# The last of four batches ranked by comparing all pairs, and new orders on all engines

## What is computed

```python
x = L0_attn_x
x = x + _L0_attn_ref(_layernorm(x), Wq, bq, Wk, bk, Wv, bv, Wo, bo, gamma, beta)
x = x + _L0_ffn_ref(_layernorm(x), w_router, w_block)
# _L0_attn_ref(x): q = elu(x@Wq+bq)+1; k = elu(x@Wk+bk)+1, each head of k divided by its norm;
#   per head (q k^T) v; y = x + attn@Wo + bo; layernorm(y)*gamma + beta
# _L0_ffn_ref(x), per batch of 1024 tokens:
scores = einsum('bld,d->bl', x, w_router)
_, top_idx = top_k(scores, 768)                 # ties: the earlier token wins
out = x.at[b, top_idx].set(gelu(x[b, top_idx] @ w_block))
```

## Time and profile before

| | us |
|---|---|
| median of 3 runs (lowest, highest) | 93.24 (93.05, 93.5) |
| the profiled execution | 93.43 |
| its span, first to last instruction | 91.7 |
| outside the span | 1.73 |
| busy: PE, DVE, ACT, POOL | 78.3, 77.8, 63.6, 65.6 |
| mean granted clock of PE | 0.884 |

### The profile page before, as it was taken

One profiled execution on the slowest core, in us unless ns is written; L12 is line 12 of the kernel. 1 busy time (PEld: TensorE's weight loads), 2 busy tenths in 40 slices (PEclk: granted clock), 3 DMA queues, 4 the chain that ended last, 5 costly groups with the idle time before them and its releaser, 6 DMA issues.

```text
span 91.7 us, 2510 instructions
## 1 busy us (share of the span) xinstructions
PE 78.3 (85%) x846; PEld 65.8 (72%) x846; DVE 77.8 (85%) x281; ACT 63.6 (69%) x187; POOL 65.6 (72%) x133
## 2 busy tenths in 40 slices
PE   4997995999999999999999999999995479985400
PEld 1356674669969979979999899989883368773300
DVE  4376999696598999999997999778879999999970
ACT  5004689999999949834998496696689997970000
POOL 5678769579799998888598888768589998600000
PEclk9999999999999999999999999999998555555555
DMA  1968979500059999993000000000000000006395
GB/s 33 283 157 298 336 275 422 223 4 7 4 63 138 139 130 131 142 145 40 0 0 7 0 0 0 0 0 11 0 0 11 0 0 0 7 0 229 123 374 199
DMA packets 8643, 9.02 MB, mean 98 GB/s; under 512 B 819, under 2 KB 6326, under 8 KB 8630
## 3 DMA queue, kind: packets, MB, share of 16 engines
q0 software_dynamic: 4160, 2.10, 21.2%
q1 hardware_dynamic: 3888, 6.49, 20.2%
q10 hardware_dynamic: 582, 0.26, 1.0%
HBM read 4.66 MB, written 2.10 MB: 74 GB/s over the span
## 4 chain that ended last, share of the span: by engine, by line
PE 48%; POOL 18%; DVE 10%; ACT 8%; DMA 6%; issue 3%; ACTq 2%; DVEq 1%
POOL x_sb L455 8%; PE bank L1251 7%; PE bank L1294 6%; PE bank L1257 6%; PE bank L1267 6%; PE bank L1295 6%; DMA off_bo<-in_L_attn_bo_dram 6%; PE bank L1317 5%; ACT norm_sb L645 5%; DVE x_sb L968 4%; POOL r L436 3%; PE bank L1219 3%; PE bank L1306 3%; POOL r L421 2%; PE bank L1335 1%
## 5 line engine op out<-in xcount | busy, mean ns | idle before, releaser
L645 ACT ACTIVATE norm_sb<-xb_sb,shift,gain 128x128 f32<-128x128 f32 x32 | 12.9, 494 | 0.5 <-POOL shift L445 0.5
L1294 PE MATMUL bank<-M_sb,qT 128*128 128x128 f32 x64 | 12.5, 277 | 0.0
L1295 PE MATMUL bank<-back,hT 128*128 128x128 f32 x64 | 12.4, 275 | 0.0
L1335 PE MATMUL bank<-ones,reach 128*16 128x1 bf16 x256 | 10.2, 164 | 1.0 <-DVE reach L922 1.0
L637 ACT ACTIVATE x_sb<-bank,r 128x128 f32<-128x128 f32 x32 | 9.7, 375 | 1.7 <-DVE s_col L897 1.6
L1344 PE MATMUL bank<-rise,rise_by 33*128 33x16 bf16 x96 | 7.0, 175 | 4.1 <-DVE rise L934 3.8
L455 POOL TENSOR_TENSOR x_sb<-x_sb,xb_sb 128x512 f32<-128x512 f32 x8 | 10.0, 1266 | 0.0
L1294 PEld LDWEIGHTS bank<-M_sb,qT 128*128 128x128 f32 x64 | 9.7, 192 | 0.2 <-ACT M_sb L606 0.2
L1317 PE MATMUL bank<-wz_c,hT 128*128 128x129 f32 x64 | 9.7, 285 | 0.0
L1295 PEld LDWEIGHTS bank<-back,hT 128*128 128x128 f32 x64 | 9.7, 192 | 0.0
L1335 PEld LDWEIGHTS bank<-ones,reach 128*16 128x16 bf16 x256 | 7.7, 88 | 2.4 <-DVE reach L922 1.3
(11 more groups left out here) (150 smaller groups left out, 216.0 us busy)
## 6 DMA issues: line engine op xcount, KB each, us to landing
xb_sb<-in_L_attn_x_dram SPq DMA_DIRECT2D x4, 512.0 KB, 7.7
xb_sb<-beta_sb POOLq DMA_DIRECT2D x4, 512.0 KB, 9.5
x_sb<-in_L_attn_x_dram SPq DMA_DIRECT2D x7, 256.0 KB, 5.9
out_dram<-x_sb SPq DMA_DIRECT2D x7, 256.0 KB, 2.4
x_sb<-in_L_attn_x_dram SPq DMA_DIRECT2D x2, 128.0 KB, 2.7
out_dram<-x_sb ACTq DMA_DIRECT2D x1, 128.0 KB, 2.5
out_dram<-x_sb SPq DMA_DIRECT2D x1, 128.0 KB, 2.5
w_sb<-in_L_attn_Wq_dram ACTq DMA_DIRECT2D x1, 64.0 KB, 2.6
```

Source lines behind the costliest of these rows:

```text
L645: last = nc.scalar.activation(norm_sb[:, t], xb_sb[:, t], ACT.Identity, bias=shift3[:, t:t + 1], scale=gain3[:, t:t + 1])
L1294: nc.tensor.matmul(o, qT[:, u, t * P:(t + 1) * P], M_sb[:, b], start=True, stop=False)
L1295: last = nc.tensor.matmul(o, hT[:, u, t * P:(t + 1) * P], back[:], start=False, stop=True)
L1335: last = nc.tensor.matmul(counts_of(s, i)[:, b - b0:b - b0 + 1], reach[:, T * b + t, :], ones16[:, 0:1], start=(t == 0), stop=(t == T - 1))
```

## The change

The diff has 1,310 lines, most of them the four rewritten lists and the banks. Its core:

```diff
-    NORM1 = "DDDDAAAA"
-    Y_STATS = "DDDAAAAA"
-    KEYS_BY = "PPPPDDPP"
+    NORM1 = "DDDDDDAA"
+    Y_STATS = "AAAAAAAA"
+    KEYS_BY = "PDPDPDPD"
...
-    RANK_SETS = ((0,), (1,), (2,), (3,))
-    ROOT_GROUPS = ((1,), (2,), (3,), (4, 5), (6, 7))
-    BUSY = 14
+    SUM_GROUPS = ((0, 1), (2, 3), (4, 5), (6,), (7,))
+    RANK_SETS = ((0,), (1,), (2,))
+    ROOT_GROUPS = ((1,), (2, 3), (4, 5), (6, 7))
+    BUSY = 11
+    def tokens(ap, b):
+        return ap[b].rearrange("(t p) d -> p t d", p=P) if b == LAST else ap[b].rearrange("(p t) d -> p t d", t=T)
+    x_v, out_v = [tokens(x, b) for b in range(B)], [tokens(out, b) for b in range(B)]
...
-            sp.dma_start(wz_sb[:, P:P + 1], w_router.unsqueeze(1)).then_inc(wz_in, 16)
             for b in range(B):
                 sp.dma_start(xb_sb[:, T * b:T * b + T, :], x_v[b]).then_inc(xb_in[b], 16)
+                if b == 0:
+                    sp.wait_ge(bo_room, 1)
+                    sp.dma_start(off_bo[:, D - 1:D], bo.unsqueeze(1)).then_inc(bo_in, 16)
+            sp.dma_start(wz_sb[:, P:P + 1], w_router.unsqueeze(1)).then_inc(wz_in, 16)
...
+            def rank_counts():
+                nc.gpsimd.memset(rise[:], 0.0)
+                nc.gpsimd.iota(lanes_i[:], pattern=[[0, B], [1, LANES]], base=0, channel_multiplier=0)
...
...
-            act.wait_ge(bo_room, 1)
-            act.dma_start(off_bo[:, D - 1:D], bo.unsqueeze(1)).then_inc(bo_in, 16)
+            def copy_s_row(h):
+                act.wait_ge(s_full, h + 1)
+                nc.scalar.copy(s_row[:, HW * h:HW * h + HW], bank_of(("s", h))).then_inc(s_row_done, 1)
+            def copy_sums(h):
+                act.wait_ge(sums_full, h + 1)
+                nc.scalar.copy(part_sums[:, HW * h:HW * h + HW], bank_of(("sums", h))).then_inc(sums_done, 1)
...
+            def compare(J, part):
+                c0, c1 = (P * (J + 1), HW) if part == 0 else (max(P * (J + 1), HW), T * P)
+                dve.wait_ge(s_row_done, part + 1)
+                nc.vector.tensor_scalar(beats[:, J, c0:c1], s_row[:, c0:c1], s_col[:, T * LAST + J:T * LAST + J + 1], None,
+                                        ALU.is_le).then_inc(beats_done, 1)
+            def compare_own(h):
+                for I in range(TH * h, TH * h + TH):
+                    last = nc.vector.scalar_tensor_tensor(out=beats[:, I, I * P:(I + 1) * P], in0=s_row[:, I * P:(I + 1) * P],
+                                                          scalar=s_col[:, T * LAST + I:T * LAST + I + 1], in1=later16[:],
+                                                          op0=ALU.is_le, op1=ALU.mult)
...
+            def score_rows(h):
+                pe.wait_ge(s_col_done, 4 * LAST + 2 * h + 2)
...
+                for t in range(TH):
+                    n = T * LAST + TH * h + t
+                    last = nc.tensor.transpose(o[:, t * P:(t + 1) * P], s_col[:, n:n + 1].to_broadcast([P, P]), ident[:])
+            def row_sums(h):
+                pe.wait_ge(beats_done, 10 if h else 7)
+                pe.wait_ge(own_done, 2)
+                for n in range(TH):
+                    J = TH * h + n
+                    for I in range(J, T):
+                        last = nc.tensor.matmul(o[:, n * P:(n + 1) * P], beats[:, J, I * P:(I + 1) * P], ident16[:],
+                                                start=(I == J), stop=(I == T - 1))
+                last.then_inc(sums_full, 1)
+            def place_columns(h):
...
+                pe.wait_ge(beats_done, 10 if h else 3)
+                pe.wait_ge(own_done, h + 1)
...
+                for n in range(TH):
+                    for J in range(a + n + 1):
+                        nc.tensor.matmul(o[:, n:n + 1], beats[:, J, (a + n) * P:(a + n + 1) * P], ones16[:, 0:1],
+                                         start=False, stop=False)
+            def place_rows(h):
+                pe.wait_ge(sums_done, h + 1)
...
+                    last = nc.tensor.matmul(o[:, n:n + 1], part_sums[:, i * P:(i + 1) * P], minus16[:], start=False,
+                                            stop=(n == TH - 1))
```

More of the change, by code:

```diff
@@ L462, in add_x1 @@
                                         ALU.add).then_inc(added, 1)
+            head_masks()
             first_masks()
-            back_masks()
             first_roots(0)
@@ L1055, in _ @@
-            y_gamma(5)
-            x1_stats(3)
-            score_cols(1, 0)
-            mask_vk(3)
-            residual(4)
-            score_cols(1, 1)
-            split_keys(0)
-            x1_stats(4)
+            score_cols(1, 0)
+            x1_stats(3)
+            mask_vk(3)
+            score_cols(1, 1)
+            residual(4)
+            split_keys(0)
+            reach_lanes(0, 0)
+            x1_stats(4)
+            y_gamma(5)
             score_cols(2, 0)
-            reach_lanes(0, 0)
+            rise_lanes(0, 0)
@@ new lines, in _ @@
+            residual(7)
+            rise_lanes(2, 0)
+            rise_lanes(0, 2)
+            reach_lanes(1, 2)
+            reach_lanes(2, 1)
+            reach_lanes(0, 3)
+            rise_lanes(1, 2)
+            score_cols(6, 0)
+            score_cols(6, 1)
+            rise_lanes(2, 1)
+            rise_lanes(0, 3)
+            reach_lanes(1, 3)
+            reach_lanes(2, 2)
+            reach_lanes(0, 4)
+            rise_lanes(1, 3)
+            rise_lanes(2, 2)
+            rise_lanes(0, 4)
@@ L1103, in _ @@
+            reach_lanes(1, 4)
+            reach_lanes(2, 3)
+            reach_lanes(0, 5)
+            rise_lanes(1, 4)
+            rise_lanes(2, 3)
+            x1_stats(7)
+            reach_lanes(2, 4)
+            reach_lanes(1, 5)
+            rise_lanes(0, 5)
+            compare_own(0)
+            low_keys(0)
+            rise_lanes(2, 4)
+            rise_lanes(1, 5)
+            reach_lanes(0, 6)
+            compare(0, 0)
             score_cols(7, 0)
-            reach_lanes(1, 3)
@@ L1135, in _ @@
+            compare(1, 1)
+            compare(2, 1)
+            low_keys(2)
+            reach_lanes(1, 7)
             rise_lanes(0, 7)
-            rise_lanes(2, 5)
-            reach_lanes(1, 7)
-            rise_lanes(3, 3)
+            reach_lanes(2, 6)
+            compare(3, 1)
+            rise_lanes(1, 7)
             ties(0)
-            reach_lanes(3, 4)
-            low_keys(2)
-            rise_lanes(1, 7)
-            reach_lanes(2, 6)
+            compare_own(1)
+            rise_lanes(2, 6)
@@ L1159, in _ @@
             merge(2)
-            reach_lanes(3, 7)
+            compare(6, 1)
             drop(2)
             merge(3)
-            rise_lanes(3, 7)
             merge(4)
-            ties(3)
+            drop_places(0)
             merge(5)
-            drop(3)
             merge(6)
+            drop_places(1)
+            merge(7)
             merge_end()
-            merge(7)
         @block.tensor
@@ L1476, in _ @@
+            move_lanes(2, 3)
+            count_lanes(0, 5)
+            transpose_x1(7)
+            move_lanes(0, 5)
+            count_lanes(2, 4)
+            count_lanes(1, 5)
+            z_half(7, 0)
+            z_half(7, 1)
+            move_lanes(1, 5)
             count_lanes(0, 6)
[L1477 to L1479 removed]
+            move_lanes(2, 4)
+            score_rows(1)
             move_lanes(0, 6)
[L1481 removed]
@@ L1508, in _ @@
-            move_lanes(3, 7)
-            rank_ties(3)
+            place_rows(0)
+            row_sums(1)
+            place_columns(1)
+            place_rows(1)
 _INS = ['L0_attn_x', 'L0_attn_Wq', 'L0_attn_bq', 'L0_attn_Wk', 'L0_attn_bk', 'L0_attn_Wv', 'L0_attn_bv', 'L0_attn_Wo',
```

617 lines of the change are left out of this document (306 added, 311 removed), and 22 rows, old and new, of the table BANK_USES.

## The result

On one chip the changed kernel took 95.14 us (median of 4 runs, 94.80 to 95.60) and the kernel before 93.37 (4 runs): a ratio of 1.0185, interval 1.0116 to 1.0255. It is slower by 1.9%. Two more comparisons with the same two kernels gave 1.0202 [1.0136, 1.0268] and 1.0166 [1.0097, 1.0236]. The profiled execution has a span of 93.6 us instead of 91.7.

What follows compares the result with a forecast made beforehand. PE was taken to bound up to 64 us, DVE from there: residual(7) 64.3 + 15.9 work + 2.0 waits = 82.2; an end chain through PE and ACT to 88.4, store to 91.3, forecast 92.8 us; 8-in-10 range 90.0 to 95.6.

Steps and rivals of the forecast that it cites:

- for waits I take 2.0: From residual(7) to compare(6,1): DVE's waiting put at 2.0 us instead of 3.5, range 1 to 3.5.
- residual(7): Its end on DVE: PE's delay of 0.7 us stays, so 64.3 us instead of 63.6.
- The comparisons need nothing from PE: After residual(7): comparisons stand where the search waits, the reason for 2.0 us of waits instead of 3.5.
- the 15.9 us of DVE's list: DVE's work from residual(7) up to compare(6,1): 15.9 of the 19.4 us it still has to do.
- The 3.5 us of waits before: Kernel before, after residual(7): of 25.2 us for 18.4 of DVE work, 3.5 went to waiting for PE's answers.
- The clock rival: PE keeps full clock to the end; shorter row_sums, z_half(7) and score_rows(1) unstretched: 1.8 us less, 91.0; chance 0.22.
- ten instructions of rank_rows: Small ACT instructions before copy_hT(2): 2.0 to 3.9 us together, 2.2 taken.
- the double rate: DVE's 10 comparisons over 3,584 columns: 3.2 us at twice the rate, taken, against 5.0 at the merge's rate.
- the four additions of POOL: Units 3 to 6, about 64.5 to 69.2 us, beside DVE's reach and rise: 0 us taken for disturbance.
- The small pieces: Last stores in 512-byte pieces: bounds 0 and 1.2 us, 0 taken.
- The start: Up to y_half(0): three idle matmuls less (0.6 us) and no PE wait for bo (0.56), together put at 0.4 us.
- the prediction's dear bound: Last stores: if every piece costs 75 ns whatever its size, the last 256 KB take 2.4 us instead of 1.2.

Runs made afterwards that it cites:

- the run with the clock held: Changed kernel with every counting matmul of the search 64 columns wide instead of 1: 93.57 us, 1.0017 of the kernel before.
- ScalarE's order alone: Changed kernel with gelu(7, 1) and norm_sum(7) ahead of the two copy_sums in ScalarE's list: 95.23 us, 1.0108 of the kernel before.
- the last run: Changed kernel with 64-column counts, reordered end lists, last batch in large pieces, unit 6's store issued by ScalarE: 92.83 us, 0.9895 of the kernel before.

## Why the prediction was wrong

**The step that failed** is "for waits I take 2.0", with which the forecast went from residual(7) to the sums, and the reason given for it, "The comparisons need nothing from PE". They do need PE: `compare` of columns 512 to 1023 reads the rows that `score_rows(1)` makes, and behind residual(7) PE must first do the transposes of unit 7, z_half(7) and then those rows; in the chain above compare(0,1) at 76.09 follows from them. The forecast had half clock from 70 us on and priced row_sums by it, but its sum holds no term for these steps and none for waiting on them. From residual(7)'s end to the start of row_sums(0) it said 15.7 us (64.3 to 80.0). The changed kernel took 18.22 (64.14 to 82.36); the run with the clock held took 16.38 (64.39 to 80.77). So 1.84 of the 2.5 us that were missing are the clock's, and 0.7 are the rest. In the forecast's own measure, the time to the end of compare(6,1) less the 15.9 us of DVE's list, the waits were 4.2 us (20.12), and 2.4 with the clock held (18.29), where it took 2.0. By the profile DVE was idle 3.10 and 1.46 us there; that is less, in part because its busy time counts each instruction's whole duration. The 3.5 us of waits before, from which the 2.0 were drawn, were in the same way what was left over of 25.2, where the profile shows 1.49 idle.

**Behind that the forecast was right, only 2.4 us late.** row_sums(0) 2.93 us (2.8 said), copy_sums(1) and then gelu(7, 1) and norm_sum(7) behind it, DVE idle ahead of unit 7's halves and released by ACT: as written, from 82.36 instead of 80.0. The last merge ended at 90.99 (88.4 said), the store took 2.6 (2.9 said). In the run with wide counts the last merge ended at 88.59 and the span at 91.4; the forecast had 88.4 and 91.3. That this is so close is partly luck: row_sums(0) started 0.8 us later than forecast there (80.77), the clock, back at 1.00 from about 83 to 86 us, made the sums shorter than the forecast's half clock does, and the median of the runs is 0.45 us above the profiled one.

**The clock rival** had the sign right and the size wrong. It read that z_half(7) and score_rows(1) "do not stretch" as a gain on the forecast, which had never charged them with a stretch. Held until 79.5 us and back from 82.9, the clock gave a time of 93.57 us, not 91.0. That its 1.8 us are also what the wide counts gave back is luck: it had made them up of shorter sums. The question to ask was not whether the clock would hold better than before but whether it would fall earlier.

**residual(7)**, 64.14 against 64.3 said, came out for another reason. ACT's small instructions cost less than taken and bo and the router weights stopped nobody, so y_half(0) started at 28.57 (30 said). PE's timeline of the changed kernel, first of y_half(0) and last of y_half(7):

```profile
28.57 0.38 PE L1370 MATMUL bank<-M_sb,qT 128*128 128x128 f32 x2
...
57.98 0.39 PE L1371 MATMUL bank<-back,hT 128*128 128x128 f32 x2
```

y_half(7) was over at 58.37, where the kernel before had 59.06: PE was ahead, not 0.7 behind. DVE's list then put reach, split_keys(2) and rise ahead of residual(7), and it started at 63.02 instead of 62.51.

**As said, or near it:** ten instructions of rank_rows in 1.6 us, from 12.54 to 14.1 (2.2 taken, and 2.0 given as the lower bound, so the bound was too high); 512-column comparisons 0.4 us apart (76.66, two in 0.86), the double rate; the four additions of POOL beside `reach` and `rise` in their 4.93 us, none beside a stretched instruction of DVE. POOL's timeline:

```profile
63.09 4.93 POOL L490 TENSOR_TENSOR x_sb<-x_sb,xb_sb 128x512 f32<-128x512 f32 x4
```

The small pieces were priced at nothing; side by side they make 0.4 us, inside the intervals. The start was to bring 0.4 us; of that the idle matmuls bring none.

**A reading that the rows do not bear** is that the idle matmuls of the earlier trace rows ran "at half clock": the profile of the kernel before gives 1.00 as the granted clock from 0 to 10 us, 0.42 us apart or not. The price taken from them held all the same: in the changed kernel the 26 matmuls of row_sums(0) take 2.72 us from start to start (82.36 to 85.08) at a granted clock of 0.50, 0.105 each where 0.107 was said.

## What to carry to other kernels

A change that moves matmuls of clock-bound length (wide ones, transposes) to where only tiny matmuls run must price every one of them at both clock levels, ahead of the bound as well as behind it, and ask whether the clock will fall earlier; a busy TensorE in the profile (4.92 of 5.00 us here) does not tell that it holds. One must also ask what the new steps read: a step that needs rows of scores needs whatever makes them. Where the clock falls, widening matmuls that are there cost less here than adding idle ones, as long as the clock then held; where it fell all the same, each of them got longer. And before an idle wait at the end is taken out, look at the stores behind it: here five merges close together gave back most of 2 us to the transfers.

## What the runs showed of the hardware

- From 65 to 70 us the granted clock fell to 0.50 with PE busy 4.92 of 5.00 us, and stayed at 1.00 with 4.91 busy where the counting matmuls had 64 columns instead of 1. With 64 columns in the kernel before it fell all the same, near 73 us instead of 70.3.
- A count of eight matmuls takes 0.34 us at either clock with 1 column, and 0.40 and 0.59 with 64.
- f32 matmuls of 65 columns with a new stationary tile each take nearly as long as those of 129: 1.97 and 2.09 us for eight, at half clock.
- Transfers in 512-byte pieces moved 304 GB/s with the engines full (89 to 91 us, ScalarE's order alone), larger ones 354 at 0.99 (87 to 89, the last run). The Trainium skill (DMA: Bandwidth & Descriptors, Specifications) puts the limit for full rate at 512 bytes; here the rows differ from it by 14%.
- q1 carried 6,208 packets in 22.0% of 16 engines over 93.6 us, where the earlier trace rows has 3,888 in 20.2% of 91.7: (329.5 - 296.4) / 2,320 = 14 ns for each packet more, not the 75 of the prediction's dear bound.
